# Separate take tables for ScalarE and VectorE at the side banks, and one normalisation for two units of heads

## What is computed

```python
qkv = (x @ w_qkv).reshape(b, n, 3, H, hd).transpose(2, 0, 3, 1, 4)
attn = jnp.einsum('bhnd,bhmd->bhnm', q, k) * scale
attn = jnp.where(attn_mask[None, None] == 0, -jnp.inf, attn)
attn = jax.nn.softmax(attn, axis=-1)
o = jnp.einsum('bhnm,bhmd->bhnd', attn, v).transpose(0, 2, 1, 3).reshape(b, n, d)
o = o @ w_proj + b_proj
ln = (o - mu) * jax.lax.rsqrt(var + LN_EPS) * ln_gamma + ln_beta
result = _layernorm(x + o + ln)
```

## Time and profile before

| | |
|---|---|
| median of 3 runs | 3419.73 us (3418.71 to 3422.11) |
| the profiled execution, its own time | 3413.86 us |
| its span (first to last instruction) | 3412.1 us |
| granted TensorE clock, mean | 0.982 of full speed |
| busy: PE, DVE, ACT, POOL | 90%, 67%, 75%, 80% |

### The profile page before, as it was taken

The page is one execution under the profiler, slowest core; times in us unless marked ns, Lnnn a source line. Parts: engine busy times, 40 slices in busy tenths (PEclk is TensorE's granted clock), DMA queues, the critical chain, the costliest instruction groups (busy, mean ns, idle before and its releaser), DMA issues.

```text
span 3412.1 us, 123185 instructions
## 1 busy us (share of the span) xinstructions
PE 3074.4 (90%) x42624; PEld 1911.3 (56%) x42624; DVE 2300.3 (67%) x4883; ACT 2543.0 (75%) x3723; POOL 2719.3 (80%) x1543
## 2 busy tenths in 40 slices
PE   6889999898998999999898998999999998998984
PEld 3555555555555555555555555556555555555552
DVE  5556667666766767767667766767676676776764
ACT  5777777777777777777787777777777787777770
POOL 3657878787887878878788887878878788887884
PEclk9999999999999999999999999999999999999997
DMA  8999999999999999999999999999999899999992
GB/s 210 179 164 181 201 182 204 187 202 189 190 204 179 206 183 202 205 177 205 183 202 194 193 203 184 207 182 202 202 181 201 179 201 196 192 201 184 207 194 72
DMA packets 2220430, 649.09 MB, mean 190 GB/s; under 512 B 2168146, under 2 KB 2168146, under 8 KB 2220372
## 3 DMA queue, kind: packets, MB, share of 16 engines
q1 hardware_dynamic: 2166372, 548.15, 86.5%
q10 hardware_dynamic: 54000, 100.16, 10.4%
HBM read 77.60 MB, written 33.55 MB: 33 GB/s over the span
## 4 chain that ended last, share of the span: by engine, by line
POOL 51%; issue 36%; SPq 8%; PE 1%; DVE 1%; DMA 1%; POOLq 1%; ACT 1%; ACTq 0%; DVEq 0%
POOL p_lo L713 45%; SPq L271 7%; POOL x_res L723 2%; POOL norm L729 2%; POOL norm L726 2%; PE proj L361 1%; DMA pt<-p_lo 1%; POOL x_res L732 1%; POOLq L712 0%; DMA x_in<-in_x 0%; ACT p L469 0%; DMA pt<-in_adj 0%; PE side L343 0%; DVE proj L650 0%; DVE x_res L655 0%
## 5 line engine op out<-in xcount | busy, mean ns | idle before, releaser
L713 POOL TENSOR_TENSOR p_lo<-p,p_hi 128x1024 f16<-128x1024 f32 x1024 | 2174.5, 2136 | 618.8 <-ACT p_hi L482 617.7
L469 ACT ACTIVATE p<-p,row_min 128x1024 f32<-128x1024 f32 x1024 | 1174.0, 1147 | 599.2 <-DVE row_min L608 598.7
L482 ACT ACTIVATE p_hi<-p 128x1024 f16<-128x1024 f32 x1024 | 1048.0, 1044 | 63.4 <-DMA pt<-p_lo 62.4
L398 PE MATMUL pv_bank<-v_both,pt 128*128 128x64 f16 x8192 | 836.3, 194 | 34.5 <-DMA pt<-p_lo 17.5
L400 PE MATMUL pv_bank<-v_both,pt 128*128 128x64 f16 x8192 | 837.0, 194 | 0.0
L399 PE MATMUL pv_bank<-v_both,pt 128*128 128x64 f16 x8192 | 837.0, 194 | 0.0
L398 PEld LDWEIGHTS pv_bank<-v_both,pt 128*128 128x128 f16 x8192 | 745.1, 99 | 131.0 <-issue 53.5
L608 DVE CUSTOM_DVE_ANT_0 p<-scores_a,mask_q 128x1024 f32<-128x1024 f32 x512 | 623.7, 1218 | 252.6 <-PE scores_b L379 204.5
L399 PEld LDWEIGHTS pv_bank<-v_both,pt 128*128 128x128 f16 x8192 | 734.6, 99 | 82.5 <-issue 3.0
L400 PEld LDWEIGHTS pv_bank<-v_both,pt 128*128 128x128 f16 x8192 | 735.3, 99 | 0.0
L608 DVE CUSTOM_DVE_ANT_0 p<-scores_b,mask_q 128x1024 f32<-128x1024 f32 x512 | 624.0, 1219 | 0.3 <-POOL p_lo L713 0.3
(11 more groups left out here) (68 smaller groups left out, 5144.6 us busy)
## 6 DMA issues: line engine op xcount, KB each, us to landing
x_res<-in_x ACTq DMA_DIRECT2D x128, 256.0 KB, 3.3
out<-x_res ACTq DMA_DIRECT2D x128, 256.0 KB, 3.2
x_in<-in_x ACTq DMA_DIRECT2D x63, 512.0 KB, 4.6
pt<-p_hi SPq DMA_TRANSPOSE x1024, 3.4
pt<-p_lo SPq DMA_TRANSPOSE x1024, 3.5
pt<-in_adj SPq DMA_DIRECT2D x8, 512.0 KB, 9.6
ot<-in_L_gnn_w_qkv SPq DMA_DIRECT2D x4, 768.0 KB, 8.7
x_in<-in_x SPq DMA_DIRECT2D x4, 512.0 KB, 7.3
```

What stands on the lines that cost most here:

```text
L398: nc.tensor.matmul(o, hi, v_hi, start=(kt == 0 and ab == 0), stop=False, skip_group_check=True)
L469: nc.scalar.activation(p32[:, slot, :], p32[:, slot, :], ACT.Exp, bias=row_min[:, slot:slot + 1], scale=-1.0, accum_out=row_sum[:, head:he ...
L482: nc.scalar.activation(p_hi[:, head % RING, :], p32[:, head % RING, :], ACT.Copy).then_inc(hi_done, 1)
L713: nc.gpsimd.tensor_tensor(p_lo[:, slot, :], p32[:, slot, :], p_hi[:, slot, :], ALU.subtract).then_inc(lo_done, 1)
```

## The change

- `TAKE_SLOT` becomes two tables. TAKE_ACT: Q1 5, V0 10, V1 10, O1 13, Q0 19, K0 and K1 29, O0 30. TAKE_DVE: Q1 6, V0 10, V1 12, O1 14, Q0 22, K0 and K1 29, O0 30. XT has its own tables, with the slots it had: 14, 16, 16, 16 for both engines.
- In ORDER one more projection matmul stands ahead of XT0 (P0 items 4 to 8 in place of 4 to 7).
- `normalise` works on two units at a time (NORM_UNITS 2): in units 1, 3, 5 and 7, at the first slot, it takes the reciprocal of four row sums and scales 256 columns of pv_bank. `times_v` waits for o_done only in even units and writes the odd unit beside the even one.
- The second row tile's norm parts move to other slots (stats 32 to 30, aggr/eps/add 35 to 33, power 37 to 35, scale 36 to 34, sum 39 to 38, stats2 40 to 38, aggr2/eps2 43 to 41, power2/out 45 to 43).
- Names that stood for XT's neighbours ("O1", "Q0", "K1") are worked out from ORDER; they come out as the same kinds.

The diff, cut to its core:

```diff
-PV_LAG, NORM_LAG = 3, 4
+PV_LAG, NORM_UNITS = 3, 2
...
-ORDER = [("Q1", 0, 12), ("V0", 0, 48), ("V1", 0, 48), ("P0", 0, 4), ("O1", 0, 4), ("P0", 4, 8), ("XT", 0, 1), ("P0", 8, 13),
-         ("XT", 1, 2), ("XT", 2, 3), ("XT", 3, 4), ("Q0", 0, 12), ("K0", 0, 12), ("K1", 0, 12), ("P1", 0, 13), ("O0", 0, 4)]
+ORDER = [("Q1", 0, 12), ("V0", 0, 48), ("V1", 0, 48), ("P0", 0, 4), ("O1", 0, 4), ("P0", 4, 9), ("XT", 0, 1), ("P0", 9,
+         13), ("XT", 1, 2), ("XT", 2, 3), ("XT", 3, 4), ("Q0", 0, 12), ("K0", 0, 12), ("K1", 0, 12), ("P1", 0, 13),
+         ("O0", 0, 4)]
...
-TAKE_SLOT = {kind: END_SLOT[kind] + 1 for kind in SIDE}
-TAKE_SLOT.update({"V0": 12, "V1": 12, "K0": 29, "K1": 29})
-NORM_SLOTS = [{"stats": 19, "aggr": 20, "eps": 20, "add": 20, "power": 21, "scale": 23, "sum": 24, "stats2": 27, "aggr2": 28,
-               "eps2": 28, "power2": 29, "out": 29},
-              {"stats": 32, "aggr": 35, "eps": 35, "add": 35, "power": 37, "scale": 36, "sum": 39, "stats2": 40, "aggr2": 43,
-               "eps2": 43, "power2": 45, "out": 45}]
+TAKE_ACT = {"Q1": 5, "V0": 10, "V1": 10, "O1": 13, "Q0": 19, "K0": 29, "K1": 29, "O0": 30}
+TAKE_DVE = {"Q1": 6, "V0": 10, "V1": 12, "O1": 14, "Q0": 22, "K0": 29, "K1": 29, "O0": 30}
+XT_ACT = [14, 16, 16, 16]
+XT_DVE = [14, 16, 16, 16]
+NORM_SLOTS = [{"stats": 19, "aggr": 20, "eps": 20, "add": 20, "power": 21, "scale": 23, "sum": 24, "stats2": 27, "aggr2":
+                28, "eps2": 28, "power2": 29, "out": 29},
+              {"stats": 30, "aggr": 33, "eps": 33, "add": 33, "power": 35, "scale": 34, "sum": 38, "stats2": 38, "aggr2":
+                41, "eps2": 41, "power2": 43, "out": 43}]
...
                 if ab == 0:
-                    wait_alone(pe, o_done, ug * UNITS + uk)
+                    if uk % NORM_UNITS == 0:
+                        wait_alone(pe, o_done, normalised(ug, uk))
...
-                ug, uk = unit_before(g, u, NORM_LAG)
-                if not active(ug, "A"):
+                ug, uk = unit_before(g, u, PV_LAG + NORM_UNITS)
+                if not active(ug, "A") or uk % NORM_UNITS:
                     return
-                dve.wait_ge(pv_done, heads(ug, uk, 2))
-                nc.vector.reciprocal(recip[:, uk % 2, :], row_sum[:, 2 * uk:2 * uk + 2]).then_inc(recip_done, 1)
+                last = uk + NORM_UNITS
+                dve.wait_ge(pv_done, heads(ug, last, 0))
+                nc.vector.reciprocal(recip[:, :], row_sum[:, 2 * uk:2 * last]).then_inc(recip_done, 1)
...
-                            if bs == TAKE_SLOT[kind]:
+                            if bs == TAKE_ACT[kind]:
                                 take(bg, kind)
...
-                            if bs == TAKE_SLOT[kind]:
+                            if bs == TAKE_DVE[kind]:
                                 take(bg, kind)
```

More of the change, by code:

```diff
@@ L29 @@
 BIAS_LO = 32
-ORDER = [("Q1", 0, 12), ("V0", 0, 48), ("V1", 0, 48), ("P0", 0, 4), ("O1", 0, 4), ("P0", 4, 8), ("XT", 0, 1), ("P0", 8, 13),
-         ("XT", 1, 2), ("XT", 2, 3), ("XT", 3, 4), ("Q0", 0, 12), ("K0", 0, 12), ("K1", 0, 12), ("P1", 0, 13), ("O0", 0, 4)]
-SIDE = ["Q1", "V0", "V1", "O1", "Q0", "K0", "K1", "O0"]
+ORDER = [("Q1", 0, 12), ("V0", 0, 48), ("V1", 0, 48), ("P0", 0, 4), ("O1", 0, 4), ("P0", 4, 9), ("XT", 0, 1), ("P0", 9,
+         13), ("XT", 1, 2), ("XT", 2, 3), ("XT", 3, 4), ("Q0", 0, 12), ("K0", 0, 12), ("K1", 0, 12), ("P1", 0, 13),
+         ("O0", 0, 4)]
+SIDE = list(dict.fromkeys(kind for kind, lo, hi in ORDER if kind[0] in "QKVO"))
+BEFORE_XT = [kind for kind, lo, hi in ORDER[:ORDER.index(("XT", 0, 1))] if kind in SIDE][-1]
+AFTER_XT = SIDE[SIDE.index(BEFORE_XT) + 1]
+NEXT_READY = [kind for kind in SIDE if kind in ("Q0", "K0", "K1")][-1]
 LENGTH = {"Q1": 12, "V0": 48, "V1": 48, "O1": 4, "Q0": 12, "K0": 12, "K1": 12, "O0": 4, "P0": 13, "P1": 13, "XT": 4}
@@ L171, in attention_block @@
         row_sum = sb("row_sum", [P, 2 * UNITS], F32)
-        recip = sb("recip", [P, 2, 2], F32)
+        recip = sb("recip", [P, 2 * NORM_UNITS], F32)
         x_res = sb("x_res", [P, 2, D], F32)
@@ L242, in turned_before, with normalised @@
             return g * (32 * 2 * UNITS // TURNED) + 32 * ((2 * u + ab) // TURNED)
+        def normalised(g, u):
+            return g * (UNITS // NORM_UNITS) + u // NORM_UNITS
         def projected(g, i):
@@ L334, in side_matmul @@
                 else:
-                    if i == 0 and known(g) and g < 0 and kind == "Q0":
+                    if i == 0 and known(g) and g < 0 and kind == AFTER_XT:
                         pe.wait_ge(w_ready, 2 * KC)
-                    if i == 0 and kind == "Q0":
+                    if i == 0 and kind == AFTER_XT:
                         wait_alone(pe, xt_dve, batch(g + 1) * T + T)
@@ L368, in unit_scores @@
                 if u == 0:
-                    wait_alone(pe, side_dve, side_done(g - 1, "K1"))
+                    wait_alone(pe, side_dve, side_done(g - 1, NEXT_READY))
                 if u == 4:
@@ L397, in times_v @@
                     v_hi, v_lo = v_both[:, kt, ab, 0:HD], v_both[:, kt, ab, HD:2 * HD]
-                    nc.tensor.matmul(o, hi, v_hi, start=(kt == 0 and ab == 0), stop=False, skip_group_check=True)
+                    nc.tensor.matmul(o, hi, v_hi, start=(kt == 0 and at == 0), stop=False, skip_group_check=True)
                     nc.tensor.matmul(o, hi, v_lo, start=False, stop=False, skip_group_check=True)
@@ L508, in body @@
                     u, j = s // QUARTERS, s % QUARTERS
-                    if known(g) and g == FIRST_GROUP and s in (XT_SLOT[0] + 1, XT_SLOT[1] + 1, XT_SLOT[2] + 2, XT_SLOT[3] + 2):
-                        pass
                     if j < 2:
@@ L516, in body @@
                         for bg, bs in slot_before(g, s):
-                            if bs == TAKE_SLOT[kind]:
+                            if bs == TAKE_ACT[kind]:
                                 take(bg, kind)
                     for i in range(T // 2):
-                        if s == XT_SLOT[i]:
+                        if s == XT_ACT[i]:
                             transposing(act, g, lambda: transposed(g, i))
-                    if known(g) and g == FIRST_GROUP and s == XT_SLOT[3]:
+                    if known(g) and g == FIRST_GROUP and s == XT_ACT[3]:
                         for kc in range(KC):
@@ L622, in normalise @@
                     wait(dve, side_ready, side_done(ug, "O1"))
-                dve.wait_ge(recip_done, ug * UNITS + (uk + 1))
-                nc.vector.tensor_tensor(o_pair[:, uk, :].rearrange("p (a d) -> p a d", a=2),
-                                        pv_bank[:, 0:P].rearrange("p (a d) -> p a d", a=2),
-                                        recip[:, uk % 2, :].rearrange("p (a o) -> p a o", o=1).broadcast_to([P, 2, HD]),
+                dve.wait_ge(recip_done, normalised(ug, last))
+                nc.vector.tensor_tensor(o_pair[:, uk:last, :].rearrange("p t (a d) -> p (t a) d", a=2),
+                                        pv_bank[:, 0:P * NORM_UNITS].rearrange("p (a d) -> p a d", d=HD),
+                                        recip[:, :].rearrange("p (a o) -> p a o", o=1).broadcast_to([P, 2 * NORM_UNITS, HD]),
                                         ALU.mult).then_inc(o_done, 1)
@@ L684, in body @@
                                     layer_norm(bg, i, part)
-                    if known(g) and g == FIRST_GROUP and s == XT_SLOT[3]:
+                    if known(g) and g == FIRST_GROUP and s == XT_DVE[3]:
                         prepare_weights()
```

17 lines of the change are left out of this document (8 added, 9 removed).

## The result

The changed kernel takes 3383.56 us, median of 6 runs (3373.52 to 3396.03), against 3419.35 for the kernel before, measured beside it (6 runs, 3414.19 to 3422.11). The ratio is 0.9898, with a 95% interval of 0.9876 to 0.9920: 35.8 us off. The forecast was 40 off (3380). The profiled execution took 3382.03 us, its span 3380.2, with the granted clock at 0.980 (0.982 before).

What follows compares the result with a forecast made beforehand. SyncE's stream of DMA transposes bounds 48 ordinary groups and runs dry in 15 fourth groups. Saving 15 x 2.7 = 40 us there gives 3413.9 - 40 + 5.9 = 3380 us, range 3356 to 3408.

Steps and rivals of the forecast that it cites:

- two regimes: SyncE's transpose stream bounds 48 ordinary groups (48.6 us); in 15 fourth groups (59.7 us) engines ahead fall behind, it runs dry.
- Rival 2: TensorE's removed waits count in every group: 48 x 1.83 + 40 = 128 us, giving 3292; chance 0.04.
- Q1 and O0, lead only: Moving these takes frees 1.8 us a group ahead of SyncE, worth 0 us in ordinary groups, only more lead.
- held high part: ScalarE's first high part of unit 2, held by an old low transpose's landing (the ring of 4 heads); 1036.30 in group 19.
- a lead of 3.2: Time in us from the end of unit 2's first high part to its transpose in fourth group 19.
- rival 4: ScalarE, held at V in slot 10, comes out 0.8 us short in 48 groups: slower, 3440; chance 0.08.
- Rival 1: Only XT0's 1.22 us wait in fourth groups counts: 15 x 1.22 = 18, giving 3401; chance 0.17.
- Unit 3 from 9.27 to 7.4: Fourth group's unit 3 on TensorE loses waits of 1.22 and 0.66 us: 1.9 saved if it starts when it did.
- Rival 3: No change: XT block and ring fix the stall's end whatever comes before; 3420, chance 0.09.
- Ordinary groups at no change: SyncE's stream covers what the change frees in ordinary groups, so they gain 0 us and stay near 48.8.
- Q0, 0 to 1 us: In fourth groups unit 4's high part starts 3.0 us later behind ScalarE's Q0 copy; cost 0, at most 1 us.
- Clock: Granted-clock drops in unit 4's block of fourth groups, 2.1 us at stake in each of 15; -18 to +12 us in the range.

Runs made afterwards that it cites:

- p1_q1_o0: The kernel before with only the Q1 and O0 takes and the second tile's norm parts moved: 3415.68 us against 3416.31.
- p3_o1: The kernel before with only the O1 take moved and one more P0 matmul ahead of XT0: 3392.93 us against 3416.31, ratio 0.9927.
- p4: The kernel before with only the normalisation of two units in one turn: 3422.21 us against 3416.31, ratio 1.0019.
- u1: The changed kernel with the V0 and V1 takes back in slot 12 on both engines: 3409.69 us, 0.9971 of the kernel before.
- p2: The kernel before with only the V0 and V1 takes moved (ScalarE 10, VectorE 10 and 12): 3416.77 us.
- c1: The kernel before with the Q1, O0 and V takes moved together, no O1 and no pair normalisation: 3404.75 us against 3420.69.
- u2: The changed kernel with the Q0 takes back in slot 20: 3381.73 us, 0.9880 of the kernel before.
- v1: The changed kernel with XT tiles spread over slots 14 to 17 and projection matmuls between them: 3377.78 us, 0.9865 of the kernel before.
- m2: The changed kernel with two empty SyncE instructions ahead of every transpose: 3377.68 us, 0.9899 of the kernel before.
- v2: v1 with GpSimd's first-tile power2 and out in slot 35, its store two slots later, ScalarE's Q0 take in 20: 3394.80 us, 0.9943.
- v3: The changed kernel with GpSimd's first-tile power2 and out in slot 35, its store two slots later, ScalarE's Q0 in 20: 3401.48 us, 0.9951.

## Why the prediction was right, point by point

**The bound, two regimes: right.** Ordinary groups did not become shorter under any edit to the engines by more than 0.15 us (48.80 to 50.16 us in the twelve kernels with full loads, the change among them, 48.95 before), while SyncE's waits in them stayed under 0.1 us in seven of these kernels and under 0.7 in all. They became shorter only when bytes were taken from beside the transposes. Rival 2 (3292) is out: the change took TensorE's waits in all from 326 to 281 us, the ordinary groups became no shorter, and the kernel measured 3383.56. In p1_q1_o0 the waits that rival 2 counts went (119.7 to 14.2 us) for a ratio of 0.9997, though most of them came back elsewhere on TensorE. The Trainium skill's *Perfetto Trace Analysis*, Optimization Strategies under Optimizing DMA Performance, sets the goal of keeping the matmul engine busy, by optimizing the engines that are "blocking the critical path" when it waits for them. In this case a wait of TensorE, even the longest one in the profile (119.7 us), did not by itself tell where that path was. A slip of the forecast: there are 49 ordinary groups, not 48; it moves nothing.

**Q1 and O0, lead only: right,** and more than the prediction said: alone that lead is not even carried to the first high part of the fourth group (3.0 us, 3.2 before). The new waits at O1 and for the normalisation are the likely reason; only with V moved as well is it 4.3.

**V: the mechanism right, both ways.** The forecast said that taking V ahead of the held high part frees the start of the XT block, and that 2 us of hold are hidden by a lead of 3.2. Both hold in the whole change. Without the lead of Q1 and O0, the cover is gone in the group behind each stall, and rival 4 is what happens, though with another matmul as the thing waited for: 2.0 us, 14 times. The 3.2 was read from a high part at the start of a fourth group, three groups behind the last stall; right behind a stall, and for the low part, the lead is smallest.

**O1 and XT0: the mechanism right.** Rival 1 priced it at 18 us with a whole wait of 1.22 gone; alone it measured 25, with an interval that holds the 18 (0.9904 to 0.9951, so 17 to 33). In its profile the 14 fourth groups gave 1.06 us each, 15 in all; the ordinary groups gave 6 more and the time up to group 6 another 7, for which the edit gives no reason. In the whole change 0.35 of the 1.22 stays in group 19, where p3_o1 has none; why was not followed up.

**Unit 3 from 9.27 to 7.4: wrong as a step.** It went to 8.36 in group 19 and from 9.42 to 8.02 on the mean, 1.4 in place of 1.9. What the forecast took from unit 3, the lead gave: unit 3 itself starts 2.2 us earlier after the group's first transpose (6.75 to 4.51), where I had put 1 us on lead plus "some more" for V. The sum for unit 4's start was then 3.6 us and for the group 3.25, inside my bounds of 1.2 to 3.5, and above the 2.7 taken: 14 groups x 0.55 = 8 us more than forecast. Rival 3, no change, is out with that.

**Ordinary groups at no change: wrong by a little, in the other direction.** They took 0.36 us more each, 15 us in all. Against that stand 8 us more than forecast from the 14 fourth groups. Start and tail gave 5.3 - 3.9 = 1.4, of which group 3 alone should have given 2.7. So the two profiles lie 31.8 us apart where the sum had 40, 8 to 9 less; the medians lie 35.8 apart, 4 less, because the profiled execution of the kernel before was 5.5 us under its median and that of the changed kernel only 1.5. That 3383.56 came so near to 3380 is thus in part luck: a gain that was too small in the sum and a loss that was not in it.

Here is the step that failed: the forecast had the ordinary groups at no change, the stream's own length as fixed. It is not. The duration of one issue was longer where the engines were further ahead, in all the runs with full loads: 1.332 to 1.346 us where a fourth group's first high part was ready 3.0 to 3.5 us early (before, p1, p3, p4, u1), 1.348 to 1.355 at 4.1 to 4.4 (after, p2, c1, u2, v1, m2), 1.362 and 1.365 at 4.8 (v2, v3).

The longer issues have a place. Summed over the four issues of a unit, the ordinary groups' means grew in units 0, 2 and 4 (5.19 to 5.37, 5.49 to 5.63, 5.28 to 5.57 us), beside ScalarE's two residual loads and a store (2.1, 26.2 and 14.0 us after the group's first transpose); units 1 and 5 lost 0.09 and 0.08, and units 6 and 7, beside the big load, had 11.49 and 11.47 together. What lengthens the issues there is not shown, nor whether the lead is its cause or comes from it.

One reading is that the DMA engines catch up while SyncE stands dry, and the following groups issue faster for it: before, the ordinary groups behind a fourth group took 48.71, 48.91 and 49.23 us in turn, after 49.32, 49.44 and 49.17. The third one is the same, and the first two lost their discount as the dry time shrank. This is argued from the numbers, not shown: v2_spread_out and v3_out, with the least dry time, are above 49.5 in all three, so something else counts too.

**Pair normalisation, 0: right for the edit alone,** open inside the whole change (see p4_pair). The estimate of 425 ns for 256 columns met 424, and the reciprocal of four took 173 where I had 160:

```profile
L633 DVE TENSOR_TENSOR o_pair<-pv_bank,recip 128x256 f32<-128x256 f32 x256 | 108.6, 424 | 9.5
...
L627 DVE RECIPROCAL recip<-row_sum 128x4 f32<-128x4 f32 x256 | 44.3, 173 | 103.5 <-PE pv_bank L410 103.5
```

That saves 3.6 - 2.4 = 1.2 us of VectorE a group, beside other work, and alone the kernel measured 1 to 12 us slower by its interval. I have no mechanism for a loss.

**Q0, 0 to 1 us: right.** The new gap ahead of the high part of unit 4 is there (1.7 us in group 19). On the mean of the fourth groups the hold costs 1.9 us at unit 4, of which 1.1 is missing again at the second gap (1.3 us with it, 2.4 without). Without it the whole takes the same time.

**Norm parts, 0:** not measured alone; they were in p1_q1_o0, which did not move.

**Clock: a small loss, not a gain.** Unit 4's block ran without a drop in 6 of 14 fourth groups before and 4 of 14 after, and took 14.18 and 14.68 us on the mean. A block without a drop took 13.1 to 13.2 us, one with a drop 15.0 to 15.3. So unit 4 took 7 us of the gain in the changed kernel's profile (14 x 0.5), some 4 of them for the two more drops; that is inside the range's allowance.

**What would show it.** SyncE's waits fell to 125.6 us (135 forecast), it did not wait in the ordinary groups of the steady part, the high parts' waits for landings rose sixfold: all as said. Three signs came only in part. Unit 3 went to 8.02 us and not 7.4, 0.35 of the 1.22 stayed in group 19, and VectorE's waits before the low parts of O0 did not go: where 2.94 stood, they are 1.51, 1.06 and 0.53 for the O0 takes of groups 19, 20 and 21, since VectorE's take of O0 is in the same slot as ScalarE's copy.

## What to carry to other kernels

Count the time of a stream that has no busy figure (the DMA issues of a queue) group by group, and separate the groups in which it runs dry from those in which it does not: in this kernel only in the former did a shorter wait of another engine give time. When a wait is gone, add up all waits of that engine before calling it removed: 92 of the 105 us had only moved, some of them to a wait that the kernel before did not have. A lead is worth something only if nothing between its source and the dry place takes it back, so two edits can be worth 0 each and 16 us together; test parts in pairs along the chain before dropping one, and the whole without each part. And look at the group right behind a stall when a wait is moved, since the cover is thinnest there.

## What the hardware showed that I had not expected

- One issue of a 128x1024 float16 DMA transpose takes 1.25 us undisturbed (5.03 us for four) and up to 1.6 beside a 512 KB load. Shrinking that load eightfold, 0.7 us of issue time an ordinary group and some 50 us of the run, was worth more than the whole change, though all loads and stores on that queue were only 10.8% of the DMA engines' span.
- Two nops on SyncE ahead of each transpose left no record in the trace, and the gaps between issues stayed at a median of 0.175 us.
- One issue took longer in the kernels whose work was ready earlier (1.338, 1.351 and 1.365 us with a lead of 3.2, 4.35 and 4.8 us), with the same bytes moved; the growth lies beside ScalarE's own loads and stores, and its cause is open.
